# Windowed attention on one Trainium2 core: a step's side products split between its middle and its end, query and key products two steps earlier, VectorE one step behind

## The reference

```
x = x + linear_attention(layernorm(x))     # first attention
x = x + experts_top2(layernorm(x)) + shared_expert
x = x + windowed_attention(layernorm(x))   # second attention: 16 heads of 16, |i-j| <= 128
x = x + expert_top1(layernorm(x))          # 8 experts, hidden 1024
```

```
energy = q k^T;  energy = -huge where |i-j| > 128
att    = softmax(energy / sqrt(256));  out = (att v) Wp^T + bp
```

## Time and profile before

| | |
|---|---|
| three timed runs | 1647.78, 1656.76, 1658.2 us (median 1656.76) |
| profiled execution, its time / its span | 1662.55 / 1660.8 us |
| busy share of the span | PE 90%, DVE 44%, ACT 27%, POOL 27% |
| chain that ended last, by engine | PE 79%, DMA 7%, ACT 5%, DVE 3%, SP's queue 3% |
| second attention: first scores / last value product | 745.35 / 1277.2 us from the span's start |
| mean granted clock of PE | 0.934 of 2.4 GHz |

### The profile page before, as it was taken

One profiled execution on the slowest core, in us unless ns is written; L12 is line 12 of the kernel. 1 busy time (PEld: TensorE's weight loads), 2 busy tenths in 40 slices (PEclk: granted clock), 3 DMA queues, 4 the chain that ended last, 5 costly groups with the idle time before them and its releaser, 6 DMA issues.

```text
span 1660.8 us, 22693 instructions
## 1 busy us (share of the span) xinstructions
PE 1493.7 (90%) x7115; PEld 997.7 (60%) x7115; DVE 734.8 (44%) x2378; ACT 446.4 (27%) x763; POOL 450.0 (27%) x533
## 2 busy tenths in 40 slices
PE   5999999999999999828899999999997279999998
PEld 3666655565777777515556666666664247667775
DVE  4354323462333333227667867867661422222221
ACT  1111111111111121103455555545543011111111
POOL 1000000003622222142444544444222033333332
PEclk8899999999999999957899999999996589999999
DMA  9200010001112212143444544534423911111110
GB/s 340 60 26 13 26 38 0 1 1 42 61 61 64 63 59 65 46 118 103 130 118 123 160 117 124 160 108 127 141 59 122 335 45 48 46 49 47 49 48 23
DMA packets 87809, 139.73 MB, mean 84 GB/s; under 512 B 10094, under 2 KB 52208, under 8 KB 87697
## 3 DMA queue, kind: packets, MB, share of 16 engines
q1 hardware_dynamic: 73856, 105.60, 20.5%
q0 software_dynamic: 12096, 32.13, 6.7%
q10 hardware_dynamic: 1744, 0.55, 0.1%
HBM read 86.46 MB, written 52.17 MB: 83 GB/s over the span
## 4 chain that ended last, share of the span: by engine, by line
PE 79%; DMA 7%; ACT 5%; DVE 3%; SPq 3%; issue 2%; POOL 1%; ACTq 0%; POOLq 0%; DVEq 0%
PE psum L632 11%; PE psum L514 10%; PE psum L831 8%; PE psum L807 8%; PE psum L611 6%; PE psum L525 5%; PE psum L680 4%; PE psum L703 4%; DMA strips<-hi 4%; PE psum L730 4%; ACT arena L989 3%; PE psum L658 3%; DMA qT<-strips 2%; PE psum L818 2%; PE psum L441 2%
## 5 line engine op out<-in xcount | busy, mean ns | idle before, releaser
L1442 DVE CUSTOM_DVE_ANT_0 work<-psum,mask 128x384 bf16<-128x384 f32 (+1 forms) x512 | 227.7, 487 | 108.7 <-PE psum L658 107.9
L989 ACT ACTIVATE arena<-psum 128x512 f32<-128x512 f32 (+1 forms) x256 | 178.1, 703 | 197.1 <-PE psum L680 196.8
L1539 POOL DMA_INDIRECT work<-normed,token_of x110 | 104.6, 951 | 416.8 <-PE psum L593 207.3
L632 PE MATMUL psum<-arena,work 128*128 x568 | 186.5, 471 | 2.9 <-ACT work L912 2.4
L658 PE MATMUL psum<-kz,qT 96*128 96x384 f32 (+1 forms) x512 | 157.1, 382 | 32.0 <-DMA qT<-strips 23.8
L514 PE MATMUL psum<-arena 128*128 128x512 f32 (+1 forms) x384 | 176.4, 602 | 0.0
L680 PE MATMUL psum<-qT,kz 100*128 100x384 f32 (+1 forms) x512 | 138.8, 347 | 28.2 <-ACT arena L989 28.1
L658 PEld LDWEIGHTS psum<-kz,qT 96*128 96x128 f32 x512 | 88.0, 198 | 94.9 <-issue 38.7
L831 PE MATMUL psum<-arena,work 128*128 x312 | 143.3, 603 | 1.2 <-ACT work L912 1.2
L807 PE MATMUL psum<-arena,work 128*128 x624 | 141.2, 379 | 1.9 <-DVE work L1494 1.9
L632 PEld LDWEIGHTS psum<-arena,work 128*128 128x128 f32 x568 | 102.9, 191 | 54.2 <-issue 5.7
(11 more groups left out here) (170 smaller groups left out, 2093.9 us busy)
## 6 DMA issues: line engine op xcount, KB each, us to landing
strips<-hi SPq DMA_DIRECT2D x64, 256.0 KB
arena<-in_w SPq DMA_DIRECT2D x16, 1024.0 KB, 12.6
kz<-strips SPq DMA_DIRECT2D x64, 192.0 KB, 3.1
qT<-strips SPq DMA_DIRECT2D x32, 384.0 KB, 4.6
results<-work SPq DMA_DIRECT2D x71, 128.0 KB, 1.7
normed<-work SPq DMA_DIRECT2D x16, 512.0 KB, 3.4
strips<-lo SPq DMA_DIRECT2D x32, 256.0 KB
X<-in_x SPq DMA_DIRECT2D x8, 512.0 KB, 9.9
```

What stands on the lines that cost most here:

```text
L632: m = e.matmul(psum[:, pair[u], 0:INTER], xsT0[:, b % 2, c * P:(c + 1) * P], wu0[:, bass.ds(x, 1), c, u * INTER:(u + 1) * INTER], start=(c ...
L989: e.activation(pT[:, j, 2 * half:2 * half + 2, 0:w], src, ACT.Exp, scale=1.0 / E ** 0.5).then_inc(p_exped, 1)
L1442: e.tensor_tensor_reduce(masked[:, n % 2, 0:w], psum[:, bank_of["scores", u, i, hd], at:at + w], mask[:, P - off:P - off + w], 1.0, MASKED ...
L1539: e.indirect_dma_start(out=xs[:, b % 3, :], out_offset=None, in_=normed[l], in_offset=bass.IndirectOffsetOnAxis(ap=token_of[:, l, b:b + 1] ...
```

## The change

The step numbers of the batch's work are moved, the order inside a step is rewritten on PE, ACT, DVE and SP, and three products are cut in two. On PE each step is now two like halves: scores, second products, then side work. Query and key products (by their two contraction chunks), transpositions (by chunk) and residuals (by token tile) put one half in the middle and one at the end of a step; the value products stay in the middle; maxima, output rows, the v products, gate and projection go to the end. ACT reads query and key products after its second exponential. DVE does what a step's products left for it one step later (`s - 1`, or the step number plus one). Query and key products move from steps -7, -5, 1, 3 to -9, -7, -1, 1; the work ahead of them moves three or four steps forward, the placement one (-3 to -4); the second residual, the norm after it, its transposition and the gate move back (31 to 35, 32 to 36, 36 to 43, 37 to 50).

```diff
-FIRST_STEP, LAST_STEP = -PRE - 6, 4 * NU + 24
+FIRST_STEP, LAST_STEP = -PRE - 10, 4 * NU + 36
+TURN_AT, GATE_AT = (-11, 43), 50
 def qk_due(step):
-    return spread(step, (-7, -5, 1, 3))
+    return spread(step, (-9, -7, -1, 1))
 def v_due(step):
-    return spread(step, (-6, -2, 2, 6))
+    return spread(step, (-8, -2, 0, 4))
 def residual_due(step):
-    return spread(step, (29, 31))
+    return spread(step, (29, 35))
@@ norm_numbers
-        for first, norm in ((32, 3), (-12, 2)):
+        for first, norm in ((36, 3), (-15, 2)):
@@ pe_turn_batch
-            for c in range(EC):
+            for c in halves:
@@ pe_qk (called with k = 0, then k = 1; the bank is filled at k = 0)
-            for k in range(EC):
-                m = e.matmul(psum[:, bk, :], w_qkv[:, k, n0:n0 + P], ...)
-            m.then_inc(bank_full[bk], 1)
+            m = e.matmul(psum[:, bk, :], w_qkv[:, k, n0:n0 + P], ...)
+            if k == EC - 1:
+                m.then_inc(bank_full[bk], 1)
@@ pe_attention, the new step
+                for half in range(2):
+                    for u, i in unit(s, 0, 4):
+                        pe_scores(e, u, i, half)
+                    for u, j in unit(s, 7, 4):
+                        pe_again(e, u, j, half)
+                    for b, t in qk_due(s):
+                        pe_qk(e, b, *divmod(t, 2), half)
+                    for norm, first in ((2, TURN_AT[0]), (3, TURN_AT[1])):
+                        for b, _ in batch(s, first):
+                            pe_turn_batch(e, norm, b, M_RING, (half,))
+                    for b, h in residual_due(s):
+                        pe_residual(e, b, h, half)
+                    if half == 0:
+                        for u, i in values_due(s):
+                            pe_values(e, u, 2 * i)
+                            pe_values(e, u, 2 * i + 1)
+                    else:
+                        ... (maxima, out_rows, v, gate, project, in this order)
@@ dve_attention
-                for u, _ in unit(s, 14, 1):
+                for b, t in qk_due(s - 1):
+                    dve_low(e, b, *divmod(t, 2))
+                for u, _ in unit(s, 15, 1):
                     dve_out_rows(e, u)
-                for b, t in v_due(s):
+                for b, t in v_due(s - 1):
                     dve_v(e, b, t)
-                for b, _ in batch(s, -9):
+                for b, _ in batch(s, TURN_AT[0] + 1):
-                for b, half in residual_due(s):
+                for b, half in residual_due(s - 1):
-                for b, i in batch(s, -PRE - 3, 2 * TPB):
+                for b, i in batch(s, -PRE - 7, 2 * TPB):
@@ pool_fetch
-            if t >= TPB and n - 2 * TPB >= 4:
+            if t >= TPB:
                 e.wait_ge(moe_added, n - 3)
@@ sync
-                for u, _ in unit(s, -3, 1):
-                    sp_place(e, u)
+                for u, _ in unit(s, 5, 1):
+                    sp_place_maxima(e, u)
                 for b, t in qk_due(s - 1):
                     sp_keep(e, b, *divmod(t, 2))
-                for u, _ in unit(s, 4, 1):
-                    sp_place_maxima(e, u)
-                for b, _ in batch(s, 31):
+                for u, _ in unit(s, -4, 1):
+                    sp_place(e, u)
+                for b, _ in batch(s, 38):
-                for b, _ in batch(s, 34):
+                for b, _ in batch(s, 41):
                     sp_normed(e, 1, b)
-                for step, xs in ((7, (0,)), (9, tuple(range(1, NX - 1))), (20, (NX - 1,))):
+                for step, xs in ((7, (0,)), (9, tuple(range(1, NX - 1))), (22, (NX - 1,))):
```

More of the change, by code:

```diff
@@ L430, in pieces, with pe_turn_batch @@
             return hot_r, hot_b
-        def pe_turn_batch(e, norm, b, ring):
+        def pe_turn_batch(e, norm, b, ring, halves=range(EC)):
             s = xn_slot(norm, b)
             e.wait_ge(xn_made, NORM[norm, b] + 1)
-            for c in range(EC):
+            for c in halves:
                 bk = next_of(ring)
@@ L748, in pe_project, with pe_residual @@
             m.then_inc(bank_full[bk], 1)
[L750 to L758, removed]
+        def pe_residual(e, b, half, t):
+            if t == 0:
+                fill(e, ("residual", b, half), next_of(M_RING))
+                e.wait_ge(oT2_made, 2 * (b + 1))
+            bk = bank_of["residual", b, half]
+            at = (2 * half + t) * P
+            for c in range(EC):
+                m = e.matmul(psum[:, bk, t * E:(t + 1) * E], oT2[:, c, at:at + P], w_p[:, c, :],
+                             start=(c == 0), stop=(c == EC - 1))
+            if t == 1:
+                m.then_inc(bank_full[bk], 1)
@@ L783, in pe_attention @@
[L783 to L789, removed]
-                for u, _ in unit(s, 4, 1):
-                    pe_maxima(e, u)
+                for half in range(2):
[15 more added lines that the diff above has]
+                    else:
+                        for u, _ in unit(s, 4, 1):
+                            pe_maxima(e, u)
+                        for u, _ in unit(s, 14, 1):
+                            pe_out_rows(e, u)
+                        for b, t in v_due(s):
+                            pe_v(e, b, t)
+                        for b, _ in batch(s, GATE_AT):
+                            pe_gate(e, 1, b, xnT[:, NORM[3, b] % 2, :, :], 3, M_RING)
+                        for b, _ in batch(s, 28):
+                            pe_project(e, b, 0)
+                            pe_project(e, b, 1)
@@ L951, in act_attention @@
                     act_exp(e, u, j, 1)
+                for b, t in qk_due(s):
+                    act_high(e, b, *divmod(t, 2))
                 for u, _ in unit(s, 4, 1):
                     act_maxima(e, u)
-                for first, norm in ((-11, 2), (33, 3)):
+                for b, _ in batch(s, 28):
+                    act_projected(e, b, 0)
+                    act_projected(e, b, 1)
+                for first, norm in ((-14, 2), (37, 3)):
                     for b, i in batch(s, first, 2):
@@ L1390, in dve_attention @@
                         dve_stats(e, t)
-                for b, i in residual_due(s):
+                for b, i in residual_due(s - 1):
                     e.wait_ge(proj_added, 2 * b + i + 1)
@@ L1394, in dve_attention @@
                         dve_stats(e, b * TPB + t)
-                for first, norm in ((-12, 2), (32, 3)):
+                for first, norm in ((-15, 2), (36, 3)):
                     for b, _ in batch(s, first):
@@ L1592, in pool_attention @@
             for s in range(FIRST_STEP, LAST_STEP):
-                for b, _ in batch(s, -9):
+                for b, _ in batch(s, -12):
                     t0 = b * TPB
@@ L1610, in pool_attention @@
                     m.then_inc(p_masked, 1)
-                for b, i in batch(s, -PRE - 6, 2 * TPB):
+                for b, i in batch(s, -PRE - 10, 2 * TPB):
                     pool_fetch(e, b * TPB + i // 2, i % 2)
-                if s == -11:
+                if s == -13:
                     pool_value_pads(e)
-                for first, norm in ((-12, 2), (32, 3)):
+                for first, norm in ((-15, 2), (36, 3)):
                     for b, _ in batch(s, first):
```

62 lines of the change are left out of this document (16 added, 46 removed).

## The result

The changed kernel takes **1675.3 us** (median of four runs, 1673.5 to 1683.4) against 1652.3 for the kernel before (four runs, 1640.0 to 1658.2): ratio 1.016, 95% interval [1.009, 1.023]. The forecast was 1634 us with a range up to 1657, so it has the wrong sign and lies outside its range. The profiled execution took 1674.8 us (span 1673.1).

What follows compares the result with a forecast made beforehand. PE was taken as the bound, with 50.8 us of work in a 63.2 us batch. Six batches -21, ramp -5 and -4, drain +6.9 sum to -23: 1639.5 profiled, 1634 us as median, range 1600 to 1657.

Steps and rivals of the forecast that it cites:

- the ramp: Start of the second attention: placement waits go, -5 us in the first sixteen steps, -4 in the next twelve.
- Gaps filled: Side work behind each half step's second products cuts their waits for ScalarE's exponential from some 10 us a batch to 0.8.
- Bank waits: PE waits at side banks that VectorE empties a step later, or for ScalarE's maxima copy: 6.2 us a batch.
- Work: PE's own work in a steady batch, unchanged in number: 50.8 us of 63.2.
- Clock: Slow clock behind the gate product in a steady batch: 1.9 us, kept unchanged.
- Drain: End of the stage: last expert's weights ahead of the last normalized rows, 2.62 MB at 380 GB/s, +6.9 us on the path.
- The one that ends slower: Rival: the two side banks become the bound, every mid-step fill waits 2.1 us, batch 71.2, +55, 1711 us; chance 0.13.
- the four fills forecast: PE's bank waits at the residual (step 3), transposition (step 11), query product (step 15) and second projection half.
- placements that still end PE's waits: Sign of a wrong forecast: PE still released by placements, where no placement wait over 1 us was expected.
- the clock under 0.95: Sign of a wrong forecast: a granted clock lower than 0.95 in the steady part.

Runs made afterwards that it cites:

- kernel 5: The changed kernel with SyncE's list reordered to maxima (step 4u+4), placement (-4), then the stores; 1636 us, 0.991 of the kernel before.
- kernel 6: kernel 5 with the last expert's weights again issued behind the last batch's normalized rows, as before the change; 1628 us, 0.987 of the kernel before.
- kernel 3: The changed kernel with the maxima's two small transfers issued by ScalarE right behind its copy, not by SyncE; 1684 us, 1.021 of the kernel before.
- kernel 9: The changed kernel, its list and drain order kept, with only VectorE's division of output rows moved ahead of the first two masks; 1664 us, 1.008.
- kernel 8: kernel 6 with VectorE's side work back in PE's own step, where it stood before the change; 1648 us, 1.001 of the kernel before.
- kernel 7: kernel 6 with VectorE dividing the output rows ahead of the step's first two masks; 1596 us, 0.966 of the kernel before.

## Why the prediction was wrong

**The step that failed** is one sentence of the ramp: "SyncE's list puts the maxima's placement first, a step later than before; two steps remain to the products that read it." It read the list by steps. First in its step means behind all of the step before, which in the new list holds the stores and the placement. The row to read was SyncE's order with its sizes: three 256 KB stores and 768 KB of placement stand ahead of the maxima, and in the rows above SyncE is still at them for 3.45 us after the copy. Cost: 26.9 us of waits in the six batches and 12.9 in the ramp, where they ate the 9 us of gain, and more clock behind them. With the list put right (kernel 5) the six batches fall by 26.3 us and the ramp by 16.2.

**Gaps filled: right in what is left, not in what it brings.** Predicted 0.8 us a batch, measured 0.3 (2.0 in six). But the prediction takes these waits down from "some 10 us" a batch, and the trace of the kernel before has 2.9 (17.4 in six), 5.0 with all of PE's other waits. The 10 is what 63.2 leaves after 50.8 of work and 1.9 of clock; part of it was work. Filling the gaps took 2.6 us a batch off the waits, 4.7 with the 2.1 by which the rest per batch fell. Without the list's loss the six batches gain 14 us (365.2 in kernel 5), not 21.

**Bank waits: right places, smaller in sum, but under-priced.** Predicted 6.2 a batch; with the late maxima out of the way they are 4.5 (10.7 + 6.9 + 6.1 of kernel 6 and 3.1 for ScalarE's copy, over six). At most, step 15 is 1.9 for 2.2, step 3 is 1.4 for 1.6, step 11 1.3 for 1.5, the projection 0.6 for 0.9. What the sum lacked is the clock behind a wait: removing 18 us of them, 12 or 13 net, gave 27 to 30.

**Work: 2 us a batch too low.** 50.8 was added up from rows; the rest per batch is 53.0, and was 55.1 before the change.

**Clock: too low.** 1.9 a batch was read from one batch and carried over; the six batches before already lost 3.2 each, and the changed kernel loses 4.6. With these four terms the batch is 53.0 + 7.7 of waits + 4.6 = 65.3 where 59.7 was forecast.

**Drain: right**, 6.4 for 6.9, and on the path: undone in 6, the stretch loses 5.6 us and the time 8.

**Rivals.** The one that ends slower had another mechanism (side banks, +55): beyond the four fills forecast none waited for VectorE, and the slowness came from the list. Of what would show it wrong, "placements that still end PE's waits" is what came, listed without a price or a chance, and so did the clock under 0.95 (0.93).

**Left open.** How much of the delay behind a batch of stores is SyncE's issue (3.45 us in the rows above) and how much the transfers' own turn was not separated: kernel 3 took away both at once and paid on ScalarE. Nor is it shown which waits are followed by the lower clock: in kernel 6 none of 1.24 to 1.26 us is, and eight of eleven from 1.37 to 1.86, five of these right behind a gate product; in kernel 9 a wait of 1.43 behind a gate product is not.

## What to carry to other kernels

When a list of DMA issues is reordered, read it as a queue with bytes in it: for every small transfer that someone waits for, name the large ones now ahead of it, and put bulk stores behind both it and the next load. When a side product is let lag, check which of its pieces the next fill of the bank waits for, and do that piece first on the emptying engine. Price a wait on TensorE together with the clock behind it, but read from the trace which waits have it: kernel 8 waits more than kernel 6 and loses less clock.

## What the runs showed of the hardware that was not expected

An issue right behind three 256 KB stores takes longer itself: two placement issues 1.96 to 2.92 us instead of 0.78, two maxima issues 2.91 instead of 1.33. Two 8 KB issues on ScalarE hold it 1.1 to 2.2 us. And in kernel 6 most waits of 1.4 to 1.9 us, eight of eleven, had the granted clock at its 1.2 GHz level behind them (a loss of 0.34 x 5 us in the rows shown); in kernel 7, with one such wait in the six batches, the clock's mean was 0.99.
